# One copy of the values instead of three in the windowed attention's products, and the loop over the turns written out

## What is computed

```python
xn = layernorm(x)
x = x + mamba(xn) + experts(xn)          # layer 0
xn = layernorm(x)
q, k, v = heads(xn @ Wq + bq), heads(xn @ Wk + bk), heads(xn @ Wv + bv)
scores = einsum('bhqd,bhkd->bhqk', q, k) / sqrt(8) + window_mask
attn = einsum('bhqk,bhkd->bhqd', softmax(scores), v)
x = x + attn @ Wo + bo + swiglu_ffn(xn)  # layer 1
```

## Time and profile before

| | |
|---|---|
| median of three runs | 1193.38 us (1186.84 to 1199.42) |
| the profiled execution | 1187.72 us |
| its span, first to last instruction | 1185.9 us |
| mean granted TensorE clock | 0.932 |
| busy: TensorE, VectorE, ScalarE, GpSimd | 915.9, 851.5, 614.4, 410.6 us |
| values matmuls (L1246) | 1024, 129.2 us busy |

### The profile page before, as it was taken

One profiled execution on the slowest core, in us unless ns is written; L12 is line 12 of the kernel. 1 busy time (PEld: TensorE's weight loads), 2 busy tenths in 40 slices (PEclk: granted clock), 3 DMA queues, 4 the chain that ended last, 5 costly groups with the idle time before them and its releaser, 6 DMA issues.

```text
span 1185.9 us, 14605 instructions
## 1 busy us (share of the span) xinstructions
PE 915.9 (77%) x4474; PEld 580.8 (49%) x4474; DVE 851.5 (72%) x1301; ACT 614.4 (52%) x1410; POOL 410.6 (35%) x234
## 2 busy tenths in 40 slices
PE   4553788847887788778879787878787888788776
PEld 2422677723544454545546455545454545455555
DVE  7772543669779877888688868887879778777242
ACT  2142556635555655564556456555646563654542
POOL 2273222234632362237223632363225432532000
PEclk9666999988999999999999899989998998999998
DMA  8174888843312332233213331342234323530000
GB/s 275 54 208 128 234 246 288 235 108 87 90 57 77 76 87 73 74 80 89 74 56 95 84 91 54 89 89 81 62 70 96 80 54 77 110 80 10 9 1 10
DMA packets 79553, 116.78 MB, mean 98 GB/s; under 512 B 4848, under 2 KB 40048, under 8 KB 79344
## 3 DMA queue, kind: packets, MB, share of 16 engines
q1 hardware_dynamic: 73184, 108.99, 34.2%
q0 software_dynamic: 6288, 6.82, 2.6%
HBM read 103.73 MB, written 12.06 MB: 98 GB/s over the span
## 4 chain that ended last, share of the span: by engine, by line
PE 40%; DVE 22%; issue 14%; POOL 12%; ACT 9%; DMA 3%; DVEq 0%; POOLq 0%; SPq 0%; ACTq 0%
PE y_bank L1157 12%; DVE hst L711 9%; PE more L1246 6%; POOL hc L1072 6%; POOL xs_d L1040 3%; DVE dBu L703 3%; ACT pexp L989 3%; PE work_l L1238 3%; POOL x_res L1056 2%; ACT pT L994 2%; PE work_l L1232 2%; PE work L1238 2%; PE work L1272 1%; DMA hst<-in_hidden 1%; PE more L1254 1%
## 5 line engine op out<-in xcount | busy, mean ns | idle before, releaser
L1072 POOL TENSOR_TENSOR hc<-hst,bcr 128x1024 f32<-128x1024 f32 x116 | 280.0, 2414 | 606.5 <-DVE dBu L703 597.8
L1157 PE MATMUL y_bank<-hc,pk 128*128 128x512 f32 x512 | 270.6, 655 | 73.4 <-POOL hc L1072 62.8
L711 DVE TENSOR_TENSOR_SCAN hst<-dA,dBu 128x1024 f32<-128x1024 f32 x128 | 291.8, 2280 | 6.5 <-ACT dA L907 5.5
L1157 PEld LDWEIGHTS y_bank<-hc,pk 128*128 128x128 f32 x512 | 100.1, 207 | 187.7 <-POOL hc L1072 87.0
L907 ACT ACTIVATE dA<-dt,neg_a 128x511 f32<-128x511 f32 x256 | 171.6, 727 | 17.1 <-DVE hst L711 13.8
L703 DVE TENSOR_TENSOR dBu<-dtu,bcr 128x1024 f32<-128x1024 f32 x128 | 158.0, 1234 | 12.7
L1246 PE MATMUL more<-vw,pT 96*128 96x99 f32 x1024 | 129.2, 277 | 35.8 <-ACT pT L994 24.5
L1246 PEld LDWEIGHTS more<-vw,pT 96*128 96x128 f32 x1024 | 119.1, 191 | 68.3 <-DVE fsg L846 31.2
L994 ACT COPY pT<-work 96x512 f32<-96x512 f32 x64 | 37.3, 582 | 155.5 <-PE work L1238 155.5
L826 DVE TENSOR_REDUCE nmax<-work 128x4 f32<-128x384 f32 x64 | 35.5, 555 | 58.9 <-PE work L1232 58.9
L994 ACT COPY pT<-work_l 96x512 f32<-96x512 f32 x64 | 37.3, 582 | 62.2 <-PE work_l L1238 62.2
(11 more groups left out here) (296 smaller groups left out, 1411.3 us busy)
## 6 DMA issues: line engine op xcount, KB each, us to landing
bcr<-bc_d SPq DMA_DIRECT2D x128, 512.0 KB, 5.0
qbd<-in_wx SPq DMA_DIRECT2D x8, 578.0 KB, 4.3
attn<-in_wx SPq DMA_DIRECT2D x8, 578.0 KB, 4.9
pT<-in_wx SPq DMA_DIRECT2D x8, 578.0 KB
kT<-in_wx SPq DMA_DIRECT2D x8, 578.0 KB, 5.0
vw<-in_wx SPq DMA_DIRECT2D x8, 578.0 KB, 4.9
xs_d<-rbuf POOLq DMA_DIRECT2D x1, 2560.0 KB, 9.8
hst<-in_hidden SPq DMA_DIRECT2D x8, 256.0 KB, 5.9
```

The source lines that it names most:

```text
L711: v.tensor_tensor_scan(hst[n % 2][:].rearrange("p h t -> p (h t)"), dA[n % 2][:].rearrange("p h t -> p (h t)"), dBu[:].rearrange("p h t -> ...
L1072: g_.tensor_tensor(hc[n % 2][:], hst[n % 2][:], bcr[n % RING][:, 1:2, :].to_broadcast([P, NH, L]), ALU.mult).then_inc(s_hc, 1)
L1157: last = t.matmul(y_bank[h][:], ident, hc[n % 2][:, h, :], start=False, stop=(n == N - 1))
```

## The change

`VREP` goes from 3 to 1: each of the eight products of a values unit streams its 33 columns once and writes 33 columns. The instruction count, the stationary operands and their loads stay the same. `iterations` writes out all turns from −1 to 9; the loop and its registers are gone, and every wait is on a constant.

```diff
-VREP = 3
+VREP = 1
...
         def iterations(eng, body):

-            body(-1, 1)
-            body(0, 0)
-            body(1, 1)
-            with eng.Fori(1, B // 2 - 1) as i:
-                body(i * 2, 0)
-                body(i * 2 + 1, 1)
-            for it in range(B - 2, B + 2):
+            for it in range(-1, B + 2):
                 body(it, it % 2)
```

## The result

| | before | changed |
|---|---|---|
| median | 1194.95 us (20 runs, 1185.03 to 1199.42) | 1201.46 us (20 runs, 1196.67 to 1219.83) |
| the profiled execution | 1187.72 us | 1204.07 us |
| mean granted clock of it | 0.932 | 0.906 |

The account below looks back on a forecast made before the run. No engine was taken as full; values products, bound by loads, were on the path about half the time. Profiled 1187.7 − 1.4 − 2.3 + 30 × 1.05 = 1215.5, so 27.8 us on the median gives 1221; range 1195 to 1254.

Parts of the forecast that it names:

- Columns don't set a unit's time: Values products: loads set the pace; only the last matmul ends some 0.05 us sooner a unit, 1.4 us off in all.
- Unrolling, −2.3: Loop's only jump back, between turns 3 and 4: writing turns out removes PE's wait, 2.3 us off, between 0 and 3.
- The clock is the cost: Values stretches: fewer streamed columns let TensorE's clock fall more often, mean grant to about 0.89, adding 30 × 1.05 us.
- Price of a fall, 1.05 us per 3.4 us of low time: Values units: each new low stretch costs 1.05 us, between 0.8 at a turn's end and 1.7 at a full PE.
- Thirty new falls: Around the 64 values units: 30 new clock falls of 3.4 us, bounds 20 and 45, adding 102 us of low time.
- the gains of 3.7: Savings of both edits: 1.4 us from sooner unit ends and 2.3 us from the jump's vanished wait.
- my columns terms: Values units with fewer columns: 1.4 us off at unit ends, 30 new clock falls at 1.05 us each added.
- The stretches outside: From the last scan to the end, outside the repeated turns: 5 to 9 us longer.
- The clock doesn't mind: Rival, values stretches: clock unaffected, only savings of 3.7 us left, 1189 to 1190 us; chance 0.11.
- Falls come, slack takes most: Rival, turns with scans: twenty falls at only 0.3 us, 1196 us, up to 1204; chance 0.09.
- Low clock feeds itself: Rival, values units: thin streams at half clock keep it low, two low stretches per fall, 1253 us and more; chance 0.07.
- Unrolling gives much: Rival, the chain's 14% issue (166 us): a tenth of it saved would be enough for 1177 us; chance 0.03.

Follow-up runs that it names:

- unroll_3copies: All turns written out with three copies kept, the unrolling alone against the kernel before: 1190.5 us, ratio 1.0002.
- unroll_5copies: All turns written out with five copies (VREP = 5), against the kernel before: 1196.6 us, ratio 1.0051.
- four_copies_filled_gap: Written out, four copies, 22 dummy matmuls ahead of one sum waiting for GpSimd in turns 1 to 6, against the kernel before: 1184.2 us, ratio 0.9954.
- after_again: The changed kernel (one copy, written out) measured again in a second comparison against the kernel before: 1203.6 us, ratio 1.0149.
- loop_1copy: Loop kept, one copy (VREP 3 to 1), the columns alone against the kernel before: 1215.6 us, ratio 1.0200.
- unroll_2copies: All turns written out with two copies (VREP = 2), against the kernel before: 1189.5 us, ratio 0.9991.

## Why the prediction went wrong, step by step

- **Columns don't set a unit's time: right.** Loads 0.111 us apart at 99, 66, 33 and 0.113 at 132 columns; the last matmul ends 0.05 us sooner. That number was right by luck: it was taken from the medians of two kinds of matmul (273 and 222 ns), and the median didn't fall.
- **Unrolling, −2.3: fails as a sum of its own.** The wait at the jump did vanish in turn 3, but unroll_3copies shows the gain given back in turns 4 and 5.
- **The clock is the cost: right.** The columns alone, with the loop and without it, made the kernel slower and raised the low time, with the loads no slower at full clock. Over the 79 executions of six kernels that were there first (before, changed, loop with one copy, written out with 2, 3 and 4; "67" in the expectation is a miscount) time is 1141.5 us + 0.28 times the low time, correlation 0.97. The line describes these kernels and is no price list: unroll_5copies lies 18 us above it and four_copies_filled_gap 9.
- **Price of a fall, 1.05 us per 3.4 us of low time, that is 0.31 a us: near.** The line gives 0.28, 0.95 us a stretch. It is an average of very unlike ones: 0 in the gap of the four-copies turn, 1.7 at a full PE, which unroll_3copies and after_again show again.
- **Thirty new falls: wrong, this is the step that failed.** Low time rose by 57 us (167 to 224), 17 stretches of 3.4 us for my 30; between the two profiled executions of before and changed it was 65 us, 19 stretches, and between unroll_3copies and after_again 45 us, 13. The term 30 × 1.05 = 31.5 becomes 17 × 0.95 = 16. With the gains of 3.7 the sum would have been +12, against +6.5 and +12.6 between the medians of the two comparisons and +16.4 between the two profiled executions. Where the count went wrong can be told. Spread evenly over the 64 values units, 30 falls are 4 in turn 1, 19 in turns 2 to 6 and 7 or 8 behind them. Measured were 5, 8 and 7 in the changed kernel against before, and 5, 5 and 4 to 5 in after_again against unroll_3copies. So outside the repeated turns the count was about right, and in them it was twice to four times too high. I judged each unit by its neighbours and added the falls to those that were there. In the repeated turns falls came and others went: turns 2 to 6, for which I had 2 to 5 us each, were 4.5 us longer together in the first pair and no longer in the second. That the turn is a cycle in which falls stand at fixed places is what the two profiles show; why they settle where they do stays open.
- **The two edits aren't independent.** With the loop kept, one copy brought 25 new stretches and 24.9 us by the medians, near the 30 falls and 30 us of my columns terms; written out it brought less. No term of mine had that. Unrolling is worth nothing at three copies and 6 to 16 us at one.
- **The stretches outside: about right.** I had 5 to 9 us more from the last scans on; 6.6 us (profiled), 6.1 (after_again). Turn 1, which gave 5.1 and 4.2 us, I hadn't named.
- **The rivals.** "The clock doesn't mind" is out: unroll_3copies against after_again differ in the columns alone. "Falls come, slack takes most" had the right number (1196 to 1204) but through a low price, where in truth the falls were fewer. "Low clock feeds itself" has something: many new low stretches are 6.8 us and more, and the end of loop_1copy has one of 27.3 us (from 1183.7); the forecast of two stretches for each of 30 falls is far off. "Unrolling gives much" is wrong at three copies.

## What to carry to other kernels

Useless columns in a load-bound matmul can pay for themselves by keeping TensorE's clock up; a kernel like this one can take them up to the distance of the loads (here 132 columns), and none should be taken away without looking at the granted clock. In a kernel with repeated turns don't add up falls unit by unit: compare low time per turn and look first at the turns that aren't repeated. Two edits that both shift when the clock falls don't add, and one profiled execution is one draw of where the falls land; compare the mean clock of many.

## What the runs showed of the hardware

- Same busy PE, same loads, a third of the columns: clock 1.00 against 0.50 behind it (330.6 to 334.0).
- Repeated turns can settle at one length with the falls at the same places of each: 122.9 us in turns 2 to 6 of after_again (one copy), in turns 3 to 6 of unroll_3copies and in turns 4 to 6 of unroll_2copies, although 120.3 is possible (four copies). Not every execution does so: the first profile of the changed kernel has 123.0 to 125.2 us. Eight operations of 0.91 us on the scans' path made the three-copies kernel no slower.
- Low clock in a gap where PE waits costs nothing: turn 4 took 120.3 us at a mean clock of 0.97 and of 1.00.
